# A decoder layer on one core: the mixture-of-experts phase with weights split in place, routing in two halves, down products two steps late and rows loaded eight tiles ahead

## What is computed

```python
E, TOP_K, H, I_MOE, I_SH = 8, 2, 256, 176, 704
shared = einsum('ti,hi->th', silu(x @ sh_gate_w.T) * (x @ sh_up_w.T), sh_down_w)
probs = softmax(x @ router_weight.T)
top_v, top_i = top_k(probs, TOP_K)
top_v = top_v / top_v.sum(-1)
combine = (one_hot(top_i, E) * top_v[..., None]).sum(1)
out = zeros_like(x)
for e in range(E):
    gu = x @ gate_up_proj[e].T
    gate, up = gu[:, :I_MOE], gu[:, I_MOE:]
    out = out + (silu(gate) * up @ down_proj[e].T) * combine[:, e:e + 1]
out = out + sigmoid(x @ shared_gate_w.T) * shared
x = layernorm(x + out)
```

## Time and profile before

| | us |
|---|---|
| three runs | 1887.63, 1892.05, 1893.84 |
| median | 1892.05 |
| the profiled execution | 1885.09 |
| its span, first to last instruction | 1883.3 |
| `phase_c` in it, from its first DMA issue | 1562.5 to 1883.3 |
| until the first routed matmul | 1562.5 to 1681.99 |
| routed tiles | 1681.99 to 1815.80 |
| second half, from the first shared matmul in it | 1815.80 to 1883.3 |

### The profile page before, as it was taken

The page is one execution under the profiler, slowest core; times in us unless marked ns, Lnnn a source line. Parts: engine busy times, 40 slices in busy tenths (PEclk is TensorE's granted clock), DMA queues, the critical chain, the costliest instruction groups (busy, mean ns, idle before and its releaser), DMA issues. The chain is left out here.

```text
span 1883.3 us, 29214 instructions
## 1 busy us (share of the span) xinstructions
PE 1723.4 (92%) x10006; PEld 1539.7 (82%) x10006; DVE 1228.9 (65%) x3392; ACT 935.0 (50%) x1702; POOL 658.4 (35%) x401
## 2 busy tenths in 40 slices
PE   6999789999999999999999999999999987737784
PEld 6888678998999899888989988998998975636673
DVE  4655467768777777877777787777778752522246
ACT  4333346556565655656565565656556542413331
POOL 1121144434333443433344343334434103560024
PEclk9999899999999999999999999999999987958898
DMA  5233643334233333523323253332334004221222
GB/s 180 69 108 107 188 104 80 69 95 113 43 105 62 80 71 93 112 44 105 62 79 74 90 110 45 105 63 80 77 86 84 15 16 127 78 82 61 68 74 90
DMA packets 123118, 159.71 MB, mean 85 GB/s; under 512 B 38432, under 2 KB 101315, under 8 KB 122851
## 3 DMA queue, kind: packets, MB, share of 16 engines
q1 hardware_dynamic: 81378, 135.77, 28.0%
q10 hardware_dynamic: 38912, 14.80, 3.8%
q0 software_dynamic: 2688, 7.34, 1.2%
HBM read 113.60 MB, written 44.29 MB: 84 GB/s over the span
## 5 line engine op out<-in xcount | busy, mean ns | idle before, releaser
L811 ACT CAST b_pT_hi<-b_turn 125x512 fp32r<-125x512 f32 (+1 forms) x768 | 406.4, 531 | 548.7 <-PE b_turn L751 529.3
L906 DVE TENSOR_TENSOR b_pT_lo<-b_turn,b_pT_hi 125x512 fp32r<-125x512 f32 (+1 forms) x768 | 477.6, 623 | 278.4 <-ACT b_pT_hi L811 272.5
L892 DVE CUSTOM_DVE_ANT_0 b_p<-b_score,b_mask_add 128x500 f32<-128x500 f32 x672 | 451.7, 673 | 52.6 <-PE b_turn L751 22.4
L751 PEld LDWEIGHTS b_turn<-b_ident,b_p 128*125 128x125 f32 x2688 | 409.8, 186 | 58.2 <-issue 1.1
L751 PE MATMUL b_turn<-b_ident,b_p 128*125 128x128 f32 x2688 | 418.7, 272 | 0.7 <-ACT b_p L817 0.7
L768 PE MATMUL b_out<-b_pT_hi,b_c_hi 125*128 125x512 f32 (+1 forms) x768 | 347.0, 452 | 10.8 <-DVE b_pT_lo L906 10.7
L817 ACT ACTIVATE b_p<-b_p,b_shift 128x1500 f32<-128x1500 f32 x224 | 347.4, 1551 | 18.3 <-DVE b_top_min L900 9.6
L1033 POOL TENSOR_TENSOR b_oT_lo<-b_oT,b_oT_hi 128x896 fp32r<-128x896 f32 x32 | 67.8, 2118 | 647.6 <-ACT b_oT_hi L839 647.6
L770 PE MATMUL b_out<-b_pT_hi,b_c_lo 125*128 125x512 f32 (+1 forms) x768 | 281.5, 366 | 0.0
L769 PE MATMUL b_out<-b_pT_lo,b_c_hi 125*128 125x512 f32 (+1 forms) x768 | 281.3, 366 | 0.0
L737 PE MATMUL b_score<-b_cT_hi,b_q_hi 128*128 128x500 f32 x672 | 264.2, 393 | 9.5 <-DVE b_cT_lo L979 9.5
(11 more groups left out here) (231 smaller groups left out, 2499.2 us busy)
## 6 DMA issues: line engine op xcount, KB each, us to landing
cT_in<-in_ctxT SPq DMA_DIRECT2D x32, 750.0 KB, 11.4
b_c_in<-in_ctx SPq DMA_DIRECT2D x32, 750.0 KB
slot_store<-b_zero SPq DMA_DIRECT2D x15, 1024.0 KB, 15.8
q_store<-a_fold_in_or_q_stage SPq DMA_DIRECT2D x16, 896.0 KB, 4.0
q_in<-q_store SPq DMA_DIRECT2D x32, 448.0 KB, 10.3
b_rden_all<-rden_store ACTq DMA_DIRECT2D x32, 256.0 KB, 5.1
b_rden_all<-rden_store ACTq DMA_DIRECT2D x32, 192.0 KB, 3.8
b_mask_in<-in_mask SPq DMA_DIRECT2D x32, 187.5 KB, 10.7
```

The source lines that it names most:

```text
L751: mm = pe.transpose(turn_bank[n % 3][0:CK, u * 128:(u + 1) * 128], p[slot % 2][:, u, c * CK:(c + 1) * CK], ident[:])
L811: act.copy(pT_hi[:, n % 3, 0:w], turn_bank[n % 3][0:CK, 0:w]).then_inc(hi_done, 1)
L892: dve.tensor_tensor_reduce(out=p[slot % 2][:, u, keys], in0=score_bank[j][:, 0:FW], in1=mask_add[:, b, keys], scale=1.0, scalar=-3.0e38, o ...
L906: dve.tensor_tensor(pT_lo[:, n % 3, 0:w], turn_bank[n % 3][0:CK, 0:w], pT_hi[:, n % 3, 0:w].bitcast(F32), ALU.subtract).then_inc(lo_done, 1)
```

## The change

- **Weights split in place.** Every piece has its own buffer (`w_in`, `e_in`, `ed_in`) and `lo` is written over it. Loads wait only for the one seven pieces earlier. POOL splits the shared pieces and two experts alone (`hi` too); for the other six ACT makes `hi` at steps 4 to 9 and DVE makes `lo` (`expert_rest`) at steps 6 to 11. No expert is left between or behind the scatters.
- **Routing in two halves.** The chain runs for tiles 0 to 7 at steps 1 to 3 and for tiles 8 to 13 at steps 3 to 5, 72 links in all. The first 16 scatters wait for the first half only. ACT takes two exponentials (`EXP_AT`), each with its table load.
- **Order of blocks** 4, 4, 4, 2. The down products come two steps late (`LAG`), `h_hi` and `h_lo` are three deep, and the first block is added to `y2` directly, at step 8.
- **Routed tiles.** `X_DEEP` is 8 (four buffers of their own, four in `y2T`), `Y_DEEP` 3, and the store reuses the register of the load.
- **Second half.** Gathers go to 28 buffers of their own in the memory of the experts' weights, seven tiles in flight. `finish` is on ACT as one activation with scale and shift, and POOL takes three instructions in place of one for each group.
- The router's weights are one DMA in place of two, and `ident` and they are issued before the tokens.

```diff
-SHARED = ((0, 4), (4, 4), (12, 2), (8, 4))
+SHARED = ((0, 4), (4, 4), (8, 4), (12, 2))
...
+        HALVES = ((0, 8), (8, 6))
+        H_DEEP, LAG, IN_FLIGHT = 3, 2, 7
+        with ExitStack() as shared_memory:
+            w_in = sb("w_in", [128, SC, W_IN + 2, 128], keep=shared_memory)
+            e_in = sb("e_in", [128, KC, EXPERTS, 2 * I_MOE], keep=shared_memory)
+            e_spare = sb("e_spare", [128, KC, EXPERTS, 2 * I_MOE], keep=shared_memory)
+            ed_in = sb("ed_in", [IH, EXPERTS, 2, F], keep=shared_memory)
...
+        x_in = [x_own[:, k, :] for k in range(4)] + [y2T_rows[:, k, :] for k in range(4)]
+        X_DEEP, Y_DEEP = len(x_in), 3
...
+        POOL_EXPERTS = 2
+        PLACES_AT = (3, 5)
+        EXPERTS_AT, DVE_EXPERTS_AT = 4, 6
+        COMBINE_AT = (0, 1, 1, 2, 2, 2, 1, 0, 1, 1, 1, 1)
...
             def load_x(s):
 
                 if s >= X_DEEP:
                     sp.wait_ge(x_turned, s - X_DEEP + 1)
-                at = sp.value_load(row[0:1, s:s + 1], min_val=0, max_val=SLOT_ROWS - T)
-                sp.dma_start(x_in[:, s % X_DEEP, :], D["slots"][bass.ds(at, T), :]).then_inc(x_loaded[s % X_DEEP], 16)
+                first_row[s] = sp.value_load(row[0:1, s:s + 1], min_val=0, max_val=SLOT_ROWS - T)
+                sp.dma_start(x_in[s % X_DEEP], D["slots"][bass.ds(first_row[s], T), :]).then_inc(x_loaded[s % X_DEEP], 16)
 
             def store_out(s):
                 sp.wait_ge(out_r_done, s + 1)
-                at = sp.value_load(row[0:1, s:s + 1], min_val=0, max_val=SLOT_ROWS - T)
-                sp.dma_start(D["slots"][bass.ds(at, T), :], out_r[:, s % Y_DEEP, :]).then_inc(out_r_stored[s % Y_DEEP], 16)
+                sp.dma_start(D["slots"][bass.ds(first_row[s], T), :], out_r[:, s % Y_DEEP, :]).then_inc(out_r_stored[s % Y_DEEP], 16)
...
+                if g in PLACES_AT:
+                    count_places(PLACES_AT.index(g))
                 hidden(g, 1)
                 if ahead:
                     turn_y2(ahead, 1)
-                if g >= 1:
-                    down(g - 1)
+                if g >= LAG:
+                    down(g - LAG)
...
+            def finish(k):
+                n = ORDER[k]
+                act.wait_ge(rstd_done, 1 + sum(first + count <= k for first, count in GROUPS))
+                act.activation(y2[:, n, :], y2[:, n, :], ACT.Identity, bias=shift_by[:, k:k + 1],
+                               scale=mv[:, k, 1:2]).then_inc(y_done, 1)
...
+            def expert_rest(p):
+                dve.wait_ge(e_hi_done, 2 * (p - SC - POOL_EXPERTS + 1))
+                for src, hi, lo in parts_of(p):
+                    dve.tensor_tensor(lo, src, hi.bitcast(F32), ALU.subtract).then_inc(e_split, 1)
...
+                if g >= LAG and g % SC == LAG and g > SC:
+                    evacuate(g // SC - 1)
                 gated(g)
...
+                if g == 7:
+                    tile_table()
+                if 0 <= g - DVE_EXPERTS_AT < EXPERTS - POOL_EXPERTS:
+                    expert_rest(SC + POOL_EXPERTS + g - DVE_EXPERTS_AT)
...
-            for p in range(SC, SC + FIRST_EXPERTS):
-                expert_rest(p)
+            for p in range(SC + POOL_EXPERTS):
+                split(p)
             for b in range(len(SHARED)):
                 scatter(b)
-                p = SC + FIRST_EXPERTS + b
-                expert_rest(p)
-            for p in range(SC + FIRST_EXPERTS + len(SHARED), PIECES):
-                expert_rest(p)
```

More of the change, by code:

```diff
@@ L1095, in phase_c @@
         PAD = 8
-        before = [sb(f"before{k}", [128, PAD + NT, EXPERTS]) for k in range(2)]
+        before = [[sb(f"before{half}{k}", [128, PAD + HALVES[half][1], EXPERTS]) for k in range(2)] for half in range(2)]
         place = sb("place", [128, NT, EXPERTS])
@@ L1426, in _ @@
                 hidden(g, 1)
-                down(g - 1)
-            down(STEPS - 1)
+                if g >= GA + LAG:
+                    down(g - LAG)
+            for g in range(STEPS - LAG, STEPS):
+                down(g)
         @block.scalar
@@ L1513, in _ @@
                     take_out(s - 2)
+            finished = 0
             for g in range(GA, STEPS):
@@ L1516, in _ @@
                 round_h(g)
+                for _ in range(FINISH_AT[g - GA]):
+                    finish(finished)
+                    finished += 1
+            for k in range(finished, NT):
+                finish(k)
         @block.vector
@@ new lines, in count_before @@
+            def count_before(half):
+                first, count = HALVES[half]
+                t, start = slice(first, first + count), PAD - half
+                assert done == PICKED[half]
+                link(dve.tensor_tensor(rest[:, t, :], pick[:, 0, t, :], pick[:, 1, t, :], ALU.add))
+                if half:
+                    link(dve.tensor_copy(before[1][0][:, start, :], before[0][1][:, PAD + HALVES[0][1] - 1, :]))
+                a, to = before[half]
+                end = PAD + count
+                link(dve.tensor_tensor(a[:, PAD:end, :], pick[:, 0, t, :], pick[:, 1, t, :], ALU.add))
+                for d in (1, 2, 4):
+                    link(dve.tensor_tensor(to[:, start:end, :], a[:, start:end, :], a[:, start - d:end - d, :], ALU.add))
+                    a, to = to, a
+                assert done == COUNTED[half]
@@ L1798, in _ @@
                 gather(k)
-                for first, count in GROUPS:
-                    if first + count == k - 1:
-                        rstd(first, count)
-            rstd(*GROUPS[-1])
+                for number in range(len(GROUPS)):
+                    if RSTD_AFTER[number] == k:
+                        rstd(number)
 def decoder_layer(nc, D):
```

374 lines of the change are left out of this document (187 added, 187 removed).

## The result

| | before | changed |
|---|---|---|
| runs, median (us) | 1892.40 (1887.63 to 1893.84, 4 runs) | 1833.22 (1826.21 to 1834.97, 4 runs) |
| ratio, 95% interval | | 0.9685 (0.9654 to 0.9715) |
| profiled execution | 1885.09 | 1833.12 |
| its span | 1883.3 | 1831.0 |
| first DMA issue of `phase_c` to the first routed matmul | 119.5 | 124.3 |

A forecast was written before the change was run, and what follows sets the result against it. No engine was full, so each of three stretches hung on waits. Savings of 21.2 us (first stretch), 58.0 (routed tiles) and 7.0 (last stretch), 86.2 in all, took 1892.05 to 1805.9 us, range 1792 to 1825.

The forecast's parts named there:

- first stretch: Until the first routed matmul, 119.5 us before: that matmul comes at 1660.8 in place of 1681.99, -21.2 us.
- Routed tiles: Middle stretch: 2.11 us a tile with loads issued further ahead, 75.8 us instead of 133.8, -58.0 us.
- rival of a register load at each tile: Routed tiles: each pays PE's register load, 2.61 us a tile, 17 us more, total 1823; chance 0.13.
- First stretch, the start of it: Before the scatters: slots out at 1609.6, first scatter 19.3 us earlier, counts waiting 1.3 and 2.8 us.
- First stretch, the scatters: POOL's 28 scatters: 35.6 us at 1.27 us each, plus 8 us for DVE's work beside them, bounds nothing to 21.2.
- the rival at the full price: First stretch: DVE holds up the scatters by 21.2 us in place of 8, total 1818.3; chance 0.12.
- chain (2): First stretch, PE and DVE: PE waits 7 us for DVE's sums at step 7; the chain ends latest, at 1660.8.
- Last stretch: After the routed tiles: DVE's list is longest, 60.5 us instead of 67.5, -7.0 us, bounds -11 and 0.
- The tail: End of the last stretch: POOL's last group, 0.70 us plus two operations of 0.2 to 0.7, then the old 4.9 us.

The follow-up runs named there:

- e9: The changed kernel with gathered tiles under way counted by four in place of seven, scatters unbroken: ratio 0.9535, first stretch 101.7 us.
- e14: The changed kernel with three pauses of five unread additions, one ahead of every seventh scatter, gathers unbroken: ratio 0.9617, first stretch 103.8 us.
- e8: The changed kernel with three expert rests moved from DVE to POOL between the scatters and the tile table behind step 8: ratio 0.9592, first stretch 100.9 us.
- e16: Kernel e8 with two gathered tiles under way in place of seven: ratio 0.9588, first stretch 104.1 us, last 65.0 us.
- e10: Kernel e8 with gathered tiles under way counted by four in place of seven: ratio 0.9572, first stretch 100.0 us.
- e5: The changed kernel run again unaltered, as a control: ratio 0.9733 to the kernel before, first stretch 124.2 us.
- e13: The changed kernel run a third time unaltered, as a control: ratio 0.9688 to the kernel before, first stretch 121.2 us.
- e15: The changed kernel with 28 plain DMAs from SP's queue to fixed rows in place of the scatters, not computing the layer: first stretch 100.9 us.
- e4: The changed kernel with three expert rests moved from DVE to POOL, one behind each of the first three groups of eight scatters: ratio 0.9559.

## Why the prediction missed

The direction was right, the size was not: 1833.2 us against 1805.9, outside 1792 to 1825. Of profiled executions it is 1833.12 against 1798.9, 34.2 us: 26.0 in the first stretch, 1.1 in the tiles, 5.5 in the last, and 1.6 outside the three. Of the 26.0, 22.6 is what parts the changed kernel from e9, which had no standstill. The other 3.4 arise ahead of step 8: e9 has its sums 81.0 us behind the stretch's start, 76.5 forecast, and takes 20.7 us from there, 21.8 forecast.

- **Routed tiles**: forecast 75.8 us, measured 76.9 (75.9 to 77.8 in all kernels with eight ahead). The reason holds: PE's transposes of successive tiles start 2.12 us apart (2.11 forecast) at a clock of 0.98. The rival of a register load at each tile, 2.61 us, falls:

```profile
1739.89 0.38 PE L1356 MATMUL c_route<-c_ident,c_x_own 128*128 128x128 f32 x2
1742.02 0.38 PE L1356 MATMUL c_turn<-c_ident,c_x_own 128*128 128x128 f32 x2
1744.13 0.38 PE L1356 MATMUL c_route<-c_ident,c_x_own 128*128 128x128 f32 x2
```

- **First stretch, the start of it**: first scatter 47.1 us behind the stretch's start forecast, 48.6 measured; counts waiting 1.3 and 2.8 us forecast, 1.59 and 3.36 measured. Right.
- **First stretch, the scatters**: 8 us were added for what DVE does beside them. In the changed kernel they run at 1.27 us throughout and end 84.4 us behind the start, not 90.7, but its DVE stood still. In e9 it did not, six of DVE's twelve rests fell beside the scatters, and of 28 only three behind the first lasted over 1.0 us (1.22, 1.09 and 1.10): 0.6 us in all behind the first. In the kernels with pauses ten or eleven rests fell beside them and the scatters lost 2.2 to 2.4 us in all, up to 0.7 us at one (e14; POOL, then DVE):

```profile
1674.06 1.63 POOL L1810 DMA_INDIRECT slot_store<-c_y,c_slot  x1 [0.30 <-issue]
...
1673.97 0.88 DVE L1693 TENSOR_TENSOR c_e_lo<-c_e_in,c_e_hi 128x704 fp32r<-128x704 f32 x1
```

  The term is 0.5 to 2.4 us in the kernels whose DVE ran on, not 8, and the rival at the full price, 1818.3, falls with it, although its time was nearer to the result, which is chance. The forecast quoted the Trainium skill, SBUF — State Buffer, "Who interferes with whom", by whose inference a `tensor_tensor` does not hold up the writing of descriptors: most scatters agree, but four of 1.35 to 1.63 us in e14, each beside such subtractions, do not: little is lost there, and not nothing. The single scatter of 2.39 us in the earlier trace rows was a poor witness: the 1.21 us operation beside it adds two tiles and does not subtract, and a subtraction of 1.30 us still ran over its first 0.4 us. What made that one long stays open. Nor did this term decide the forecast, which went by chain (2).
- **First stretch, the failed step**: the working asked what DVE does to the scatters, and never what the scatters do to the others. Its chain (2) gave PE, ACT and DVE their usual pace beside 28 indirect DMAs in a row. Before, they came in runs of at most eight with POOL's rests of 3 us between the earlier trace rows; the change took these rests away and so made the run. Where the standstill is absent or the run is broken the forecast of 98.3 us came out as 100.0 to 105.2 (e9 101.7, where PE waits 6.04 us at step 8 for the 7 forecast). With it, 121 to 125: a term of some 20 us that the sum had at nothing.
- **Last stretch**: 60.5 us forecast; 58.8 to 61.7 without the standstill, 66.0 to 71.7 with it. It is the same step that failed: the gathers, too, were reckoned as if nothing else slowed beside them. The tail is as reckoned, POOL's three small operations and then ACT (changed kernel):

```profile
1824.84 0.70 POOL L1829 TENSOR_TENSOR c_mv<-c_mv,c_half 128x2 f32<-128x2 f32 x1 [4.10 <-DVE c_mv L101]
1825.61 0.19 POOL L1831 TENSOR_TENSOR c_shift_by<-c_mv 128x2 f32<-128x2 f32 x1
1825.89 0.19 POOL L1833 TENSOR_SCALAR c_shift_by<-c_shift_by 128x2 f32<-128x2 f32 x1
1826.12 1.09 ACT L1515 ACTIVATE c_y<-c_y,c_shift_by,c_mv 128x256 f32<-128x256 f32 x2 [2.34 <-POOL c_shift_by L1833]
```

The forecast as a ratio was 0.9545, and e9, the changed kernel but for a wait that does not bind, gave 0.9535 (0.9491 to 0.9578) in a group without the standstill. The ranges left no room for a price that no row of before shows. Where the standstill shows, e8 (0.9592 beside 0.9733 for the changed kernel) and e16 (0.9588 beside 0.9688) are faster than the changed kernel. Where it doesn't, neither was run; e10, which is e8 with a wait that does not bind, has 0.9572 (0.9532 to 0.9612) beside the 0.9535 of e9, which can't be told apart.

## What to carry to other kernels

When an edit takes an engine's other work from among its indirect DMAs, the DMAs close up into one long run, and the trace of before shows nothing of what that does. Break such a run every seven or eight with work of 3 us or more, best with work that is needed anyway; it cost 2 to 4 us here where it was not needed, which is no more than single profiles differ by, and saved 17 to 23 where it was (in e8 and e16 the later table is part of that). And if a cure seems to work, look whether an untreated place of the same run shows the illness: four kernels of ours were "cured" in a group that never had it.

## What was not expected of the hardware

- Beside a run of some 13 or more indirect DMAs at 1.27 us each, PE, ACT and DVE can come nearly to a stop, PE issuing an instruction each 0.7 to 2.8 us, at a DMA share of 0.3. That it goes when the run is broken was shown in two groups (e8 beside e5; e14 and e16 beside e13), and that the bytes of the rows do not bring it in one (e15 beside e13). What it is that runs short stays open. PE's rows that wait for nothing look like a lack of instructions, but the trace shows no transfer of instructions from 1628 to 1679, and in e9 one of 16 KB, at 1646.37, lies amid 28 unbroken scatters without a standstill.
- In the profiled executions it shows in all kernels of a group that have such a run, or in none: groups 0, 2 and 4 against 1, 3 and 5. Of the executions without a profile nothing is known. Groups 1 and 4 ran on the same chip, so the chip is not what decides. What does stays open, and so does how long a run may be; the first fourteen gathers were long enough for it to begin.
- A DVE subtraction with both inputs in SBUF took 3.58 us (e4) and 3.79 us (e8) in place of 0.69 where two such subtractions of POOL, 1.7 and 1.3 us, began beside it: it ended 0.5 us behind the second, so it waited for both, not for one. The Trainium skill, SBUF — State Buffer, "Who interferes with whom", has DVE and POOL contend where DVE has two inputs in SBUF and POOL reads it, and the trace agrees; that two of POOL's instructions in a row are waited out is this trace's.
